# A compensated softplus: the rounding of 1 + e on ScalarE instead of VectorE, in three of eight mixers

## What is computed

```python
dt = jax.nn.softplus(jnp.einsum('blr,re->ble', dt_lo, W_dt) + b_dt)
A = -jnp.exp(A_log)
def step(h, inp):
    dt_t, B_t, C_t, u_t = inp
    dA = jnp.exp(dt_t[..., None] * A)
    h = dA * h + (dt_t * u_t)[..., None] * B_t[:, None, :]
    y_t = jnp.einsum('ben,bn->be', h, C_t)
    return (h, y_t)
```

## Time and profile before

| | |
|---|---|
| median of 3 runs | 776.4 us (775.49 to 776.85) |
| profiled execution: its own time | 773.7 us |
| its span, first to last instruction | 771.9 us |
| mean granted TensorE clock | 0.996 |
| TensorE busy (products) | 710.7 us, 92% of the span |
| VectorE busy | 685.3 us, 89% |
| ScalarE busy | 640.6 us, 83% |
| GpSimd busy | 610.4 us, 79% |

### The profile page before, as it was taken

The page is one execution under the profiler, slowest core; times in us unless marked ns, Lnnn a source line. Parts: engine busy times, 40 slices in busy tenths (PEclk is TensorE's granted clock), DMA queues, the critical chain, the costliest instruction groups (busy, mean ns, idle before and its releaser), DMA issues. The chain is left out here.

```text
span 771.9 us, 21849 instructions
## 1 busy us (share of the span) xinstructions
PE 710.7 (92%) x8031; PEld 403.9 (52%) x8031; DVE 685.3 (89%) x1138; ACT 640.6 (83%) x1282; POOL 610.4 (79%) x599
## 2 busy tenths in 40 slices
PE   7889999998999989999999999979998999888798
PEld 4676644644555346547555356445464453343356
DVE  6988339989999999999999899999999999899973
ACT  4778688999989999998889999988979866856633
POOL 5013347888998999788898789999999999999960
PEclk9999999999999999999999999999999999999989
DMA  6000014533524161423425171525261525254410
GB/s 211 3 3 2 3 46 152 164 97 107 186 71 138 45 200 63 135 77 107 128 64 183 46 232 58 178 92 174 69 192 46 178 83 178 91 171 144 143 42 28
DMA packets 45003, 83.56 MB, mean 108 GB/s; under 512 B 5081, under 2 KB 5730, under 8 KB 44898
## 3 DMA queue, kind: packets, MB, share of 16 engines
q1 hardware_dynamic: 44898, 82.18, 33.5%
HBM read 71.15 MB, written 11.01 MB: 106 GB/s over the span
## 5 line engine op out<-in xcount | busy, mean ns | idle before, releaser
L1820 POOL TENSOR_TENSOR d<-d,cr 128x1024 f32<-128x1024 f32 x128 | 300.1, 2355 | 17.4 <-DVE d L1315 6.9
L1632 ACT ACTIVATE ps<-dt,An 128x512 f32<-128x512 f32 x252 | 172.2, 696 | 36.7 <-DVE d L1315 36.0
L1315 DVE TENSOR_TENSOR_SCAN d<-ps,hl,d 128x512 f32<-128x512 f32 x128 | 157.2, 1262 | 5.0 <-ACT ps L1632 4.3
L1315 DVE TENSOR_TENSOR_SCAN d<-ps,d 128x512 f32<-128x512 f32 x128 | 149.9, 1205 | 7.2 <-ACT ps L1632 6.9
L886 PE MATMUL ps<-h,w 128*128 128x512 f16 (+1 forms) x512 | 115.8, 379 | 6.6 <-DVE h L1243 6.3
L1303 DVE TENSOR_TENSOR d<-ps,du 128x512 f32<-128x512 f32 x173 | 111.6, 671 | 3.8 <-ACT ps L1615 2.2
L1806 POOL TENSOR_TENSOR d<-du,br 128x512 f32<-128x512 f32 x79 | 99.9, 1276 | 5.7 <-PE ps L981 4.1
L886 PEld LDWEIGHTS ps<-h,w 128*128 128x128 f16 x512 | 48.1, 99 | 76.1 <-DVE h L1243 17.8
L981 PE MATMUL ps<-d,cst 128*32 128x512 f32 x512 | 68.1, 604 | 3.2 <-POOL d L1820 3.2
L897 PEld LDWEIGHTS ps<-w,h 128*128 128x128 f32 x496 | 58.2, 192 | 8.3 <-issue 5.5
L897 PE MATMUL ps<-w,h 128*128 128x128 f32 x496 | 60.6, 277 | 0.8 <-ACT h L1529 0.8
(11 more groups left out here) (186 smaller groups left out, 1373.0 us busy)
## 6 DMA issues: line engine op xcount, KB each, us to landing
cr<-bcd SPq DMA_DIRECT2D x64, 256.0 KB, 3.3
br<-bcd SPq DMA_DIRECT2D x64, 256.0 KB, 3.1
dt<-dtd SPq DMA_DIRECT2D x64, 256.0 KB, 3.9
du<-dud SPq DMA_DIRECT2D x64, 256.0 KB, 3.6
dtd<-sR SPq DMA_DIRECT2D x16, 256.0 KB, 3.0
dud<-sE SPq DMA_DIRECT2D x16, 256.0 KB, 2.3
X<-in_x SPq DMA_DIRECT2D x8, 256.0 KB, 6.4
out<-X SPq DMA_DIRECT2D x3, 512.0 KB, 4.0
```

The costliest lines, as they stand in the source:

```text
L1315: eng.tensor_tensor_scan(d, banks[u % NG][:, :], d, hl[:, r:r + 1] if m % 2 else 0.0, ALU.mult, ALU.add).then_inc(v_sc, 1)
L1632: eng.activation(banks[u % NG][:, :], src[:, :], ACT.Exp, scale=An[:, g:g + 1]).then_inc(s_da, 1)
L1820: eng.tensor_tensor(d, d, CR[k % NC][:, :].unsqueeze(1).to_broadcast((128, n, 512)), ALU.mult).then_inc(p_cm, n)
```

## The change

In the last three mixers, blocks n = 10 to 15, `dt_v` is gone from VectorE's queue. In its place ScalarE runs two functions of the kind Copy with a constant bias: sT = sE + 1 between Exp and Ln, and sT = sT - 1 behind Ln. Blocks 0 to 9 stay as they are. The places of all other steps stay. The counts of `s_md` (five functions a block from n = 10 on) and `v_md` (one instruction a block) are adapted everywhere they are waited for, and GpSimd's first instruction waits for ScalarE's last function instead of VectorE.

```diff
+ROUNDED = 10
+def by_s(n):
+    return max(0, n - ROUNDED)
...
-    (BLOCKS, 'dr_v dt_d dt_p dt_s dt_t dt_v du_d du_p mu_s mu_t'),
+    (BLOCKS, 'dr_v dt_d dt_p dt_s dt_t du_d du_p mu_s mu_t'),
+    (BLOCKS[:ROUNDED], 'dt_v'),
...
             def dt_d(m, eb):
                 n = 2 * m + eb
-                eng.wait_ge(v_md, 2 * n + 2)
+                eng.wait_ge(v_md, 2 * (n + 1) - by_s(n + 1))
...
-                bank = bank_of["md", m, eb] = turn((v_md, 2 * n + 2))
+                bank = bank_of["md", m, eb] = turn((v_md, 2 * (n + 1) - by_s(n + 1)))
...
                     eng.wait_ge(l_du, 16 * n)
-                    eng.wait_ge(v_md, 2 * n)
+                    eng.wait_ge(v_md, 2 * n - by_s(n))
...
                 eng.activation(sE[:, :], bank_of["md", m, eb][:, :], ACT.Abs).then_inc(s_md, 1)
-                eng.wait_ge(s_md, 3 * n + 1)
+                at = 3 * n + 2 * by_s(n)
+                eng.wait_ge(s_md, at + 1)
                 eng.activation(sE[:, :], sE[:, :], ACT.Exp, scale=-1.0).then_inc(s_md, 1)
-                eng.wait_ge(s_md, 3 * n + 2)
+                eng.wait_ge(s_md, at + 2)
+                if n < ROUNDED:
+                    eng.activation(sL[:, :], sE[:, :], ACT.Ln, bias=1.0).then_inc(s_md, 1)
+                    return
+                eng.wait_ge(p_md, 3 * n)
+                eng.activation(sT[:, :], sE[:, :], ACT.Copy, bias=1.0).then_inc(s_md, 1)
                 eng.activation(sL[:, :], sE[:, :], ACT.Ln, bias=1.0).then_inc(s_md, 1)
+                eng.wait_ge(s_md, at + 3)
+                eng.activation(sT[:, :], sT[:, :], ACT.Copy, bias=-1.0).then_inc(s_md, 1)
...
             def dt_p(m, eb):
                 n = 2 * m + eb
-                eng.wait_ge(v_md, 2 * n + 1)
+                at = 3 * n + 2 * by_s(n)
+                if n >= ROUNDED:
+                    eng.wait_ge(s_md, at + 5)
+                else:
+                    eng.wait_ge(v_md, 2 * n + 1)
                 eng.tensor_tensor(sT[:, :], sE[:, :], sT[:, :], ALU.subtract).then_inc(p_md, 1)
-                eng.wait_ge(s_md, 3 * n + 3)
+                eng.wait_ge(s_md, at + (4 if n >= ROUNDED else 3))
...
             def du_p(m, eb):
                 n = 2 * m + eb
-                eng.wait_ge(v_md, 2 * n + 2)
+                eng.wait_ge(v_md, 2 * (n + 1) - by_s(n + 1))
```

More of the change, by code:

```diff
@@ L313 @@
         667132],
-    "dt_v": [110219, 127934, 177635, 191916, 263347, 280126, 346610, 381692, 434996, 453666, 495919, 517134, 581827, 601682, 654268,
[1 row of a table removed]
+    "dt_v": [110219, 127934, 177635, 191916, 263347, 280126, 346610, 381692, 434996, 453666],
     "du4_d": [119140, 120370, 120985, 124337, 142430, 145593, 148114, 148729, 186640, 187255, 188485, 191782, 222600, 223748, 234345,
```

## The result

The changed kernel takes 779.25 us (median of 20 runs, 775.35 to 781.55) against 775.33 for the kernel before on the same chip (20 runs, 773.13 to 778.86). The ratio is 1.0043, 95% interval 1.003 to 1.0057: slower, by some 3.3 us by the ratio and 3.9 by the medians. The forecast was +2.7 us and 779.1, slower with a chance of 0.55. The profiled execution has a span of 778.7 us against 771.9, but that 6.8 is no measure of the change, as will be seen.

A forecast was written before the change was run, and what follows sets the result against it. VectorE was taken to set the pace, GpSimd close behind. Block terms -0.35 + 1.06 + 1.06 + 0.7 + 1.0 - 0.35 gave +3.1, less 0.4 absorbed: +2.7 us, 779.1 against the median of 776.4; range 773.8 to 781.8.

The forecast's parts named there:

- absorbed: Term of the sum: later waits, in block 12 and between blocks 13 and 14, take up 0.4 us of the delay.
- What bounds: 490 to 740 us: VectorE sets the pace, GpSimd close behind, but shares can't tell if ScalarE is ahead at each block.
- The price of a Copy: ScalarE, blocks 10 to 15: each added Copy costs 0.53 us of queue, 1.06 a block, with ends of 1.02 and 1.56.
- dearer Copy: Rival: a Copy on ScalarE takes 778 ns, so the sum is +5.4 us, 781.8; chance 0.09.
- Blocks 11, 12, 13: Scan in 11 waits for its decay, +1.06; sR in 12 for GpSimd's add, +1.06; second scan in 13, +0.7.
- rival "absorbed": One block's delay eats the next stretch's wait; blocks 14 and 15 leave +0.65 us, 777.1, no change; chance 0.20.
- Block 14: Copy of B behind Ln on ScalarE comes later, three drives wait for it: +1.0 us.
- Block 10: Scan can begin 0.45 us earlier, but GpSimd gains only the 0.36 it waited for the tensor_scalar: -0.35 us.
- Block 15: Scan could begin 0.6 us earlier, but GpSimd has to follow, so the same -0.35 us as block 10.
- The hold by GpSimd: VectorE's tensor_scalar seems held until GpSimd's product ends: 1.43 us in block 10, 1.84 in 15, against 0.41 in 11.
- VectorE's time counts: Rival: the 5.3 us removed count whole, only blocks 11, 12, 14 pay 1.06 each: -2.1 us, 774.3; chance 0.21.

The follow-up runs named there:

- second profile of before: The kernel before, unchanged, profiled and timed once more: 776.49 us against 776.48, ratio 0.9998.
- removal alone: Kernel before without the tensor_scalar in blocks 10 to 15, nothing in its place, rounding correction left out: 773.22 us against 776.13, ratio 0.9961.
- functions alone: Kernel before keeping its tensor_scalar, with two Copies added on ScalarE ahead of Ln in blocks 10 to 15: 781.16 us against 776.13, ratio 1.006.
- GpSimd's rounding: Kernel before with the rounding made by a GpSimd tensor_scalar in blocks 10 to 15, no added ScalarE function: 783.06 us against 775.76, ratio 1.0082.
- filler apart: The full change with 18 instead of 12 warm products ahead of block 14's wait for sR: 779.54 us against 775.42 for before, ratio 1.0048.
- blocks 10 and 15 alone: Kernel before with the change made in blocks 10 and 15 only: 774.69 us against 776.13, ratio 0.9983.
- less filler: Kernel before with 6 instead of 12 warm products in the row ahead of block 14's wait for sR: ratio 1.001.
- blocks 11 to 13: Kernel before with the change made in blocks 11, 12 and 13 only: 778.18 us against 775.76, ratio 1.0019.
- blocks 11 to 14: Kernel before with the change made in blocks 11 to 14 only: 780.02 us against 776.13, ratio 1.0047.
- block 14 alone: Kernel before with the change made in block 14 only: 776.55 us against 775.76, ratio 1.0002.

## Why the prediction was right, and where its sum was off

Against the second profile of before, whose falls of the clock lie where after's do, term by term (us):

| block | forecast | full change | what was off |
|---|---|---|---|
| 10 | -0.35 | +0.15 | gained at the scan, lost at the scores |
| 11 | +1.06 | +1.06 | nothing |
| 12 | +1.06 | +1.01 | nothing |
| 13 | +0.7 | | |
| absorbed | -0.4 | +0.32 (with 13) | nothing |
| 14 | +1.0 | +1.92 | the clock |
| 15 and tail | -0.35 | -0.87 | hold and clock |
| sum | +2.7 | +3.59 | |

- **What bounds.** That shares don't decide was right. Against the second profile of before, VectorE's busy time fell by 4.6 us (685.9 to 681.3; said: 5.3), its idle time grew by 8.5 (88.9 to 97.4; said: 8), and ScalarE's busy time rose by 5.6 (said: 7). The removal alone, without any new cost, is worth 3.0, and the functions alone cost 4.7.
- **The price of a Copy.** 0.53 each was right (1.05 a pair). With it the dearer Copy falls. The estimate of 1.2 us for one Copy that I drew from the Trainium skill ("Trainium Architecture — The Big Picture", section "The five engines, in one table") is twice the measured 0.61 to 0.63. Against the free tensor_scalar of 0.41 a Copy is 1.5 times as long, within the page's "up to" 3.
- **Blocks 11, 12, 13.** Right in place, size and released engine. Scans waited 2.23 and 1.36 (said: 1.6 and 1.4), sR 2.93 (said: 2.8). The wait in block 11 is longer than said since it was longer already: in the second profile of before this scan waits 0.71 us and not the 0.27 of the earlier trace rows, and 0.71 + 1.06 + 0.43 of removed tensor_scalar is 2.20. In block 12 ScalarE's decays are as late as GpSimd's sum, so both queues hold the price; the forecast named only the sum.
- **Absorbed.** 1.66 became 1.17 at the wait between 13 and 14: 0.5 taken up, where I had taken 0.4 in all. The wait of 2.60 stayed 2.59, so it moved along, as argued against the rival "absorbed". That rival falls: stretches 11 to 12 and 12 to 13 keep all of their +1.0.
- **Block 14.** The mechanism (drives wait for the copy of B, 1.64 us) was right, and this is the term that was mis-sized: 1.0 became 1.9. I followed the delay on VectorE and ScalarE and not to sR's other reader. TensorE waits for sR to free its bank, and 1.76 us of idle time ahead of it stood in the trace of before. With 1.3 us more the clock fell in the profiles of all six kernels that have functions or GpSimd's rounding there, filler apart (3.08 to 3.45 us idle), and in none of the other eight (1.76 to 2.04). With filler in the gap the term is +1.01.
- **Block 10.** The scan came 0.5 earlier behind its Abs (0.34 against the second profile), as said, and with the two functions in ScalarE's queue it was worth nothing: VectorE then waits for TensorE's scores, 0.44 in after. The gain needed TensorE to be early too.
- **Block 15.** The gain was larger than said. Behind its own Abs the scan comes 0.67 us earlier, in after and with blocks 10 and 15 alone. That is the whole 0.6 that the prediction read off the rows and then halved, for GpSimd would have to follow; it needn't have. Another 0.14 of the term lies at the scan of the tail (1.43 in the second profile, 1.29 in after), and so with the clock.
- **The hold by GpSimd.** In block 10 the tensor_scalar is 1.43 or 1.44 us in all seven profiles that have it, in block 11 0.41 or 0.43. In block 15 it is 1.84 or 1.85 in both profiles of before, with less filler and with blocks 11 to 13, but 0.56, 0.86 and 0.42 with blocks 11 to 14, block 14 alone and the functions alone, where block 14's change shifts the engines against each other. Wherever it is long it ends 0.27 to 0.29 us behind GpSimd's running tensor_tensor. So it is a hold and no cost of the operation. The Trainium skill's rule that the prediction quotes ("SBUF — State Buffer", section "Who interferes with whom") fits these rows.
- **"VectorE's time counts"** was the strongest rival with 0.21, and it falls: of 5.3 us, 3.0 count with nothing in their place, and the stretches behind blocks 11 to 14 ask for 4.3 back.

The +2.7 stands close to the measured +3.3 in part by luck, because errors cancel: +0.9 in block 14 and +0.5 in block 10 against -0.5 in block 15 and the tail. That 779.1 is within 0.2 us of the measured 779.25 is luck too: it was counted from 776.4, the median of three executions, where 20 gave 775.33, and 775.33 + 2.7 would be 778.0.

## What to carry to other kernels

Before you move work to an idle engine, look at where its idle time lies: here ScalarE waited 31 us for scans, and still the whole added microsecond reached VectorE in three of six blocks and a third of it in a fourth. Follow a delay to every reader of the late tile, TensorE above all, and ask what idle piece it lengthens; the price of a delay can be twice its length when the clock falls behind it. And compare by stretches between fixed marks, with a second profile of the unchanged kernel: 0.05 us can be read there, where the medians of whole runs can't tell 1 us. Timed executions say more when those with the same granted clock are compared.

## What the runs showed of the hardware that was not expected

- TensorE's clock: in block 14 a single idle piece of 3.08 us ahead of two products came with a fall from 1.00 to the lower level (a mean of 0.72 over 6 us with block 14 alone), while 1.76 us, or 1.40 and 1.76 with 1.47 us of work between them, did not. Near 736 us shorter pieces came with one: in before 1.96 and 1.69 us with 0.59 us of products between.
- Two places (near 510 to 524 and near 736 us) lose clock without any change of the code, and by amounts that differ between executions: 1.47 or 2.74 us for the same six products, and 4.54 to 6.02 us for the same 14.
- A tensor_scalar of VectorE that starts while GpSimd runs its tensor_tensor of 2.36 us ends 0.28 us behind it: it takes up to 1.84 us instead of 0.41.
- On GpSimd a tensor_scalar of two additions over 128x512 takes 1937 ns, while one of a multiplication and an addition over the same shape (L1836 of before) took 695 ns. Whether the kinds of operation or where the operands come from make the difference was not tried.
- Functions of ScalarE that don't read each other's result start 0.52 to 0.54 us apart at a length of 0.61 to 0.63; one that reads the one just before starts 0.66 behind it (505.30 to 505.96).
